# A state-space scan laid out as 8 channels x 16 states per tile instead of 128 channels, and routing counts in two matmuls

## The chip, the cores and the metric

One core of a Trainium2 chip runs the whole program. The metric is the device time of one execution in microseconds (us). The times of the kernel before are three runs: 4642.11, 4643.89 and 4647.07, median 4643.89.

## The reference

A network of four layers on 16 sequences of 256 tokens and 128 channels (4096 tokens). The change is in layer 2, which has two parts. Its first part is a selective state-space block; for a normalised input `xn` of 128 channels:

```python
xz = xn @ W_in; xi, z = jnp.split(xz, 2, axis=-1)          # 256 channels each
xc = silu(causal_conv4(xi) + conv_b)
dt_lo, Bm, Cm = jnp.split(xc @ W_xp, [8, 8 + 16], axis=-1)
delta = softplus(dt_lo @ W_dt + dt_bias)
def step(h, inp):                                          # h: (batch, 256 channels, 16 states)
    dt_t, B_t, C_t, u_t = inp
    h = h * exp(dt_t[..., None] * A) + (dt_t * u_t)[..., None] * B_t[:, None, :]
    return h, einsum('bdn,bn->bd', h, C_t)
y = (scan(step) + xc * D_skip) * silu(z)
out = y @ W_out
```

Its second part is a mixture of 16 experts (128 to 512 to 128, ReLU), two selected per token. The routing gives every token a place in its two experts' rows, for which it counts, per expert, the tokens before it.

## The kernel before

Tokens are worked on in 8 chunks of T = 512 (two sequences of 256). All tensors have channels on the 128 partitions and tokens along the free axis, in float32. The program is written out by hand for five engines (PE, ACT, DVE, POOL and SP for transfers), each with its own in-order list and semaphores between them. It runs layers 0 and 1, then `layer2_route`, `layer2_mix`, and layer 3.

**`layer2_route` (L752)** goes through the chunks in a loop of 9 rounds, one round overlapping the gate and norm of chunk i with the routing of chunk i-1. PE (L834 to L843): `turn(i)`, `logits(i-1)`, the two norm products of chunk i, and last `counts(i-1)` (L821), which counts with 10 products of 16 columns for the tokens before and 4 for the total. DVE (L915 to L932): `select(i-1)`, `gate_finish(i)`, then `place(i-1)` (L893), which waits for the counts, then `ln_vector(i)`. POOL scatters the rows with eight indirect transfers per chunk when the places are there.

**`layer2_mix` (L987)** is the stage of the scan. Each chunk has NS = 16 steps, one per state; the tile of a step is 128 channels x 512 tokens, for two halves of the 256 channels side by side (1024 columns). In every step:

- PE `spread_states(k, n)` (L1072): two products of 32 rows spread row n of B and row n of C over 128 partitions, into banks 0 and 1. They wait for the drive product and C's copy of the step before.
- ACT `decay(k, n)` (L1187): two exponentials exp(delta x A) from SBUF into DA, then C's spread copied from PSUM to CN.
- DVE `drive(k, n)` (L1297): DB = DU x B's spread (out of PSUM, 1024 columns), then the scan (L1308) over 1024 columns.
- POOL (L1355 to L1368): state x C for the near half (L1355), for the far half (L1362), and the far half added up (L1364). DA, DB and ST have two buffers each.
- PE `add_near(k, n-1)` (L1084): a product with the identity adds up the near half in bank 5.

In steps 3 to 12 of a chunk (FIRST = 3, SLOTS = 10) one expert tile of 128 rows runs beside: PE transposes the rows (`tile_rows`, L1099), computes the output of the tile before (`tile_out`, L1113) and this tile's hidden values (`tile_hidden`, L1107), and ACT copies and applies ReLU between them. SP loads the tile j when the output of tile j-2 is done. Each step also carries one part of `head(k+1, n)`: the norm, input projection, convolution, silu, projection to B, C and delta, and the softplus of the next chunk; on ACT, steps 7, 11 and 12 have most of it. The order on every engine is step by step:

```python
for n in range(NS):
    decay(k, n)                                      # ACT; spread_states on PE, drive on DVE
    j = SLOTS * k + n - FIRST
    if FIRST <= n < FIRST + SLOTS: tile_rows(j)
    if FIRST < n <= FIRST + SLOTS: tile_out(j - 1)
    if FIRST <= n < FIRST + SLOTS: tile_hidden(j)
    if k + 1 < CHUNKS: head(k + 1, n)
```

DVE takes the sums of chunk k-1, gates them (`gated`, L1311) after step 0 of chunk k, and adds the input (`add_input`, L1322) after step 1.

`keep_warm` (L125) in other stages issues bf16 products of two constants, `identb` and `windowb`, of 128x128 and 128x512; their result is not read.

Of the kernel before, what the change touches and what calls it, by code (L numbers as in the profile page):

```python
# [13 lines left out]
SEQ = 256  # L14
# [31 lines left out]
def columns(parts):  # L46
    at, out = 0, {}
    for name, width in parts:
# [8 lines left out]
          ("window", 4 * 128), ("expert", E2), ("tile", TILES), ("full", TOKENS // 128), ("eps", 1), ("one", 1), ("aeps", 1), ("pow", 1), ("lnnorm", 1)]  # L57
# [4 lines left out]
W2 = [("g", 1), ("b", 1), ("win", 2 * 2 * 128), ("conv", 2 * TAPS), ("cb", 2), ("xp", 2 * (DTR + 64)), ("dt", DI),  # L62
# [689 lines left out]
def layer2_route(nc, c, w, r, soft, x_mid, s_mid, y_mid, xn_mid, xs_mid, PB):  # L752
    with ExitStack() as ctx:
# [13 lines left out]
        with nc.Block() as block:  # L767
# [31 lines left out]
            def _(pe):  # L799
# [21 lines left out]
                def counts(k):  # L821
                    pe.wait_ge(s.route_ready, k + 1)
                    if k:
                        pe.wait_ge(s.count_taken, k)
                    for t in range(TT):
                        o = PB[:, 6, t * E2:(t + 1) * E2]
                        nc.tensor.matmul(o, c.before, b.OC[:, t, :], start=True, stop=t == 0)
                        for u in range(t):
                            nc.tensor.matmul(o, c.ones, b.OC[:, u, :], start=False, stop=u == t - 1)
                    for t in range(TT):  # L830
                        last = nc.tensor.matmul(PB[:, 6, TT * E2:TT * E2 + E2], c.ones, b.OC[:, t, :], start=t == 0, stop=t == TT - 1)
                    last.then_inc(s.count_ready, 1)

                for i in range(CHUNKS + 1):  # L834
                    if i < CHUNKS:
                        turn(i)
                    if i:
                        logits(i - 1)
                    if i < CHUNKS:
                        pe.wait_ge(s.x_gated, i + 1)  # L840
                        ln_tensor(nc, pe, s, c, of(i).X, PB[:, 1:5], i)
                    if i:
                        counts(i - 1)  # L843
# [22 lines left out]
            def _(dve):  # L866
# [47 lines left out]
                link(nc.vector.tensor_copy(r.base[:], c.expert))  # L914
                for i in range(CHUNKS + 1):  # L915
# [10 lines left out]
                    if i:  # L926
                        place(i - 1)
                    if i < CHUNKS:
# [3 lines left out]
                        ln_vector(nc, dve, s, c, of(i).XN, PB[:, 1:5], link, i).then_inc(s.xn_ready, 1)  # L932

                nc.vector.tensor_scalar(tails[:], r.base[:], 0.0, None, ALU.add).then_inc(s.tails_ready, 1)
# [3 lines left out]
                link(nc.vector.tensor_tensor(b.CT[:], r.base[:], c.expert, ALU.subtract))  # L938
# [41 lines left out]
            "xm_ready xz_ready xi_copied conv_done silu_x silu_z xd_ready dtl_copied bc_copied dt_ready dt_raw dt_exp dt_u dt_log delta_ready "  # L980
            "pads_set b_ready c_ready c_copied drive_ready decay_ready state_ready near_ready far_ready near_added near_summed far_summed "
            "sums_taken y_gated mamba_ready s_added ")
SLOTS = TILES // CHUNKS
FIRST = 3


def layer2_mix(nc, c, w, wf, r, xn_mid, s_mid, xs_mid, ys_mid, PB):  # L987
    with ExitStack() as ctx:
        s = semaphores(nc, ctx, MIX_SEMS)
        b = buffers(nc, ctx, "l2", XN=[3, T], XM=[T], XI=[2, NB, TAPS - 1 + SEQ], XC=[2, 2, T], ZS=[2, 2, T], DL=[2, 2, T], DU=[2, 2, T],  # L990
                    BC=[2, T], EE=[2, T], UU=[2, T], DTL=[T], CN=[2, T], DA=[2, 2, T], DB=[2, 2, T], ST=[2, 2, T],
                    CA=[2, T], CB=[T], YA=[T], YG=[2, T], SO=[T], WB=[2, W2ROW], XR=[2, 128], XT=[128], H=[4, 128], YO=[2, 128])
        xn_loaded, tile_loaded, tile_stored = (s.xn_loaded0, s.xn_loaded1, s.xn_loaded2), (s.tile_loaded0, s.tile_loaded1), (s.tile_stored0, s.tile_stored1)
        B1 = 2 * HID2
        B2 = B1 + 4

        with nc.Block() as block:
            @block.sync
            def _(sp):
# [38 lines left out]
            def _(pe):  # L1038
                def head(k, step):
                    p = k % 2  # L1040
                    if step == 0:
                        pe.wait_ge(xn_loaded[k % 3], 16 * (k // 3 + 1))
                        if k:
                            pe.wait_ge(s.dt_raw, k)
                        nc.tensor.matmul(PB[:, 6, :], c.centre, b.XN[:, k % 3, :], start=True, stop=True).then_inc(s.ln_centred, 1)
                    elif step == 1:
                        pe.wait_ge(s.ln_square, k + 1)
                        nc.tensor.matmul(PB[:, 7, :], c.mean, c.lnsq[:], start=True, stop=True).then_inc(s.ln_var, 1)
                    elif step == 4:
                        pe.wait_ge(s.xm_ready, k + 1)  # L1050
                        for h in range(2):
                            nc.tensor.matmul(PB[:, 6 + h, :], w.win[:, h * 128:(h + 1) * 128], b.XM[:], start=True, stop=True).then_inc(s.xz_ready, 1)
                    elif step == 5:
                        pe.wait_ge(s.xi_copied, k + 1)
                        for h in range(2):
                            nc.tensor.matmul(PB[:, 6 + h, :], w.win[:, (2 + h) * 128:(3 + h) * 128], b.XM[:], start=True, stop=True).then_inc(s.xz_ready, 1)
                    elif step == 9:
                        pe.wait_ge(s.silu_z, 2 * k + 2)
                        pe.wait_ge(s.silu_x, 2 * k + 2)
                        for h in range(2):  # L1060
                            nc.tensor.matmul(PB[0:DTR, 6, :], w.xp[:, h * 72:h * 72 + DTR], b.XC[:, p, h, :], start=h == 0, stop=h == 1)
                        for h in range(2):
# [1013 lines left out]
```

## Time and profile before

| | |
|---|---|
| median of three runs | 4643.89 us |
| profiled execution, its own time | 4658.04 us |
| its span | 4656.4 us |
| mean granted clock of TensorE over the span | 0.793 |
| busy, share of the span | PE 74%, DVE 57%, ACT 39%, POOL 33% |
| layers 0 and 1, up to | about 1120 us |
| `layer2_route` | 1120 to 1347 us |
| `layer2_mix` | 1347 to 2351 us, first scan at 1391.9 |
| layer 3 | from 2351 us |

The profile is of one execution, so its rows are to be held against 4658, not against the median. "Granted clock" is a share of 2.4 GHz; TensorE runs at either 1.2 or 2.4 GHz, and a mean of 0.75 over a stretch is half of it at either. A float32 product appears as two PE instructions, so a count of 8 is four products.

### The profile page before, as it was taken

Reading aid. Unit: us, or ns where it says so; the run is one execution under the profiler, and the core shown is the slowest. Engines: PE = TensorE matmul, PEld = TensorE weight load, DVE = VectorE, ACT = ScalarE, POOL = GpSimd, SP = SyncE. Lnnn points to the kernel's source line nnn. Section 1 sums busy time; section 2 is a strip of 40 time slices with the busy share of each in tenths; the row PEclk is TensorE's granted clock in tenths of the full one; section 3 lists DMA queues with packets and bytes.
Section 4 is the critical chain, followed back from the end, with each engine's and each line's share of the span. In section 5 each row is a group of like instructions: output and inputs, shape, how many; then the busy total and the mean of one; then the engine's idle time right before and its main releaser. Section 6 shows DMA issues by size and latency. Waiting matters only on the chain. (4 is left out here: it accounts for less than half of the span.)

```text
span 4656.4 us, 50785 instructions
## 1 busy us (share of the span) xinstructions
PE 3423.9 (74%) x17802; PEld 1842.6 (40%) x17802; DVE 2642.8 (57%) x3696; ACT 1828.2 (39%) x3692; POOL 1538.3 (33%) x1231
## 2 busy tenths in 40 slices
PE   5888888883538788788757677676776857778587
PEld 3444444441424344344323334333343334343343
DVE  3444444442547777777655566555665656556565
ACT  3333333331214444444424434344343434434344
POOL 0000000003316665656644253332533424334242
PEclk8888888885557777777768879688797988959789
DMA  1000000002212222222100000000000000000000
GB/s 80 7 7 7 7 7 7 7 5 74 72 42 63 67 67 67 67 67 59 59 16 5 8 1 5 8 5 8 1 5 8 5 8 1 8 6 5 8 1 8
DMA packets 70704, 111.46 MB, mean 24 GB/s; under 512 B 8640, under 2 KB 46016, under 8 KB 69952
## 3 DMA queue, kind: packets, MB, share of 16 engines
q1 hardware_dynamic: 65088, 97.47, 6.5%
q0 software_dynamic: 5376, 11.02, 0.9%
q8 instruction: 123, 2.02, 0.2%
q14 instruction: 117, 0.96, 0.1%
HBM read 81.71 MB, written 26.74 MB: 23 GB/s over the span
## 5 line engine op out<-in xcount | busy, mean ns | idle before, releaser
L369 ACT ACTIVATE l_PT<-PB 128x512 f32<-128x512 f32 x512 | 277.9, 594 | 539.1 <-PE PB L280 539.1
L280 PE MATMUL PB<-l_QM,l_KP 32*128 32x256 f32 x2048 | 375.2, 497 | 131.6 <-DVE l_QM L418 75.9
L407 DVE TENSOR_REDUCE keep_MXP<-PB 128x4 f32<-128x1024 f32 x256 | 301.5, 1220 | 106.8 <-PE PB L253 106.8
L280 PEld LDWEIGHTS PB<-l_QM,l_KP 32*128 32x128 f32 x2048 | 241.3, 243 | 256.4 <-ACT l_PT L369 99.9
L1308 DVE TENSOR_TENSOR_SCAN l_ST<-l_DA,l_DB 128x1024 f32<-128x1024 f32 x128 | 313.7, 2451 | 42.0 <-ACT l_DA L1196 32.8
L1355 POOL TENSOR_TENSOR l_CA<-l_ST,l_CN 128x512 f32<-128x512 f32 x128 | 182.6, 1426 | 397.6 <-DVE l_ST L1308 346.0
L703 POOL MEMSET l_KV<- 128x4 f32 x8 | 0.8, 105 | 918.5 <-POOLq L109 918.5
L1515 POOL TENSOR_TENSOR l_PT<-l_PT,l_PEN 128x512 f32<-128x512 f32 x168 | 212.5, 1284 | 184.5 <-ACT l_PT L369 184.5
L1089 PE MATMUL PB<-l_CA,consts 128*128 128x512 f32 x256 | 199.2, 872 | 71.4 <-POOL l_CA L1355 71.4
L1779 POOL TENSOR_TENSOR l3f_SQ<-l3f_RW 128x512 f32<-128x512 f32 x128 | 146.8, 1147 | 302.4 <-ACT l3f_RW L1645 302.4
L1302 DVE TENSOR_TENSOR l_DB<-l_DU,PB 128x1024 f32<-128x1024 f32 x128 | 155.4, 1214 | 154.1 <-PE PB L1079 153.4
L1583 PE MATMUL PB<-l3f_QK 64*64 64x128 f32 x2048 | 159.3, 301 | 80.5 <-DVE l3f_QK L1719 80.5
L1788 POOL TENSOR_TENSOR l3f_PP<-l3f_PP,l3f_RS 128x512 f32<-128x512 f32 x128 | 133.1, 1040 | 251.2 <-DVE l3f_RS L1737 251.2
L1079 PE MATMUL PB<-l_BC,consts 32*128 32x512 f32 x256 | 180.9, 792 | 42.7 <-DVE l_DB L1302 22.0
L253 PE MATMUL PB<-l_KP,l_QP 32*128 32x256 f32 x2048 | 198.0, 514 | 15.6 <-issue 15.6
L1362 POOL TENSOR_TENSOR l_CB<-l_ST,l_CN 128x512 f32<-128x512 f32 x120 | 208.8, 1740 | 0.0
L1670 ACT ACTIVATE l3f_PP<-PB,l3f_MN 128x128 f32<-128x128 f32 x512 | 146.4, 368 | 157.6 <-DVE l3f_MN L1731 157.6
L294 PE MATMUL PB<-l_PT,keep_VT 128*32 128x256 f32 x2048 | 170.6, 490 | 35.2 <-POOL l_PT L1515 19.2
L418 DVE TENSOR_TENSOR l_QM<-l_QP,PB 128x256 f32<-128x256 f32 x128 | 53.9, 421 | 237.0 <-PE PB L262 233.5
L1364 POOL TENSOR_TENSOR l_YA<-l_YA,l_CB 128x512 f32<-128x512 f32 x120 | 184.2, 1535 | 9.4
L1401 POOL TENSOR_SCALAR l_T<-l_AJ,l_GI 128x256 f32<-128x256 f32 x16 | 18.4, 1147 | 504.0 <-DVE l_AJ L1491 504.0
L1081 PE MATMUL PB<-l_BC,consts 32*128 32x512 f32 x256 | 182.1, 797 | 0.0
(416 smaller groups left out, 7934.3 us busy)
## 6 DMA issues: line engine op xcount, KB each, us to landing
l_WB<-in_w2f_dram SPq DMA_DIRECT2D x80, 578.0 KB, 3.4
l_XR<-xs_mid SPq DMA_DIRECT2D x80, 64.0 KB, 3.5
ys_mid<-l_YO SPq DMA_DIRECT2D x80, 64.0 KB, 3.3
w3fs<-in_w3f_dram SPq DMA_DIRECT2D x1, 3125.0 KB, 16.6
keep_XI<-in_x_dram SPq DMA_DIRECT2D x9, 256.0 KB, 3.0
x_mid<-keep_X SPq DMA_DIRECT2D x9, 256.0 KB, 3.0
s_mid<-keep_S SPq DMA_DIRECT2D x9, 256.0 KB, 2.0
keep_SI<-s_mid SPq DMA_DIRECT2D x9, 256.0 KB, 2.6
```

The costliest lines, as they stand in the source:

```text
L253: last = nc.tensor.matmul(PB[:, r, qt * SEQ:(qt + 1) * SEQ], b.QP[rows, a, q0:q0 + 128], b.KP[rows, a, i, sq * SEQ:(sq + 1) * SEQ], start= ...
L280: last = nc.tensor.matmul(PB[:, 4 + u % STBANKS, kt * SEQ:(kt + 1) * SEQ], b.KP[rows, a, i, k0:k0 + 128], b.QM[rows, n % 2, :], start=True ...
L369: nc.scalar.activation(b.PT[:, u % PSLOTS].rearrange("p k q -> p (k q)"), PB[:, 4 + u % STBANKS, :], ACT.Exp).then_inc(s.exp_done, 1)
L407: nc.vector.tensor_reduce(dst[:, 2 * pair:2 * pair + 2, :, 16 + n % 2], PB[:, 2 * pair:2 * pair + 2, :].rearrange("p r (t k) -> p r t k", ...
L1079: nc.tensor.matmul(PB[:, 0, :], c.ident[0:32, n:n + 1].broadcast_to([32, 128]), b.BC[0:32, k % 2, :], start=True, stop=True).then_inc(s.b_ ...
L1081: nc.tensor.matmul(PB[:, 1, :], c.ident[32:64, 32 + n:33 + n].broadcast_to([32, 128]), b.BC[32:64, k % 2, :], start=True, stop=True).then_ ...
L1089: last = nc.tensor.matmul(PB[:, 5, :], c.ident, b.CA[:, g % 2, :], start=n == 0, stop=n == NS - 1)
L1308: nc.vector.tensor_tensor_scan(b.ST[:, g % 2].rearrange("p k t -> p (k t)"), b.DA[:, g % 2].rearrange("p k t -> p (k t)"), b.DB[:, g % 2]. ...
L1355: nc.gpsimd.tensor_tensor(b.CA[:, g % 2, :], b.ST[:, g % 2, 0, :], b.CN[:, g % 2, :], ALU.mult).then_inc(s.near_ready, 1)
L1362: nc.gpsimd.tensor_tensor(b.CB[:], b.ST[:, g % 2, 1, :], b.CN[:, g % 2, :], ALU.mult).then_inc(s.far_ready, 1)
L1364: last = nc.gpsimd.tensor_tensor(b.YA[:], b.YA[:], b.CB[:], ALU.add)
L1515: nc.gpsimd.tensor_tensor(pt, pt, b.PEN[:, 2 * sq:2 * sq + 2, :], ALU.mult).then_inc(s.weighed_pool, 1)
```

## The change

**The scan's layout.** A step now works on a pair of tiles of 8 channels x 16 states (128 partitions) x 512 tokens; 16 pairs (PAIRS) cover the 256 channels. delta and delta x u are spread from 8 channels to 128 partitions by PE (`rowsel`, four products of 32 rows per step: two of delta for the next pair into banks 0 and 1, two of the drive for this pair into banks 2 and 3). B and C are spread once per chunk (`statesel`) and copied to BT and CT by ACT. ACT's exponentials read PSUM. DVE multiplies the drive's spread with BT and scans. POOL makes one product per step, state x CT over 1024 columns in place, in a ring of four buffers, and once per chunk the product delta x xc. PE adds up the 16 states of two pairs with four products of 32 output rows, every second step. Ahead of each step's spreads PE issues FILL = 4 bf16 products of the constants.

```diff
+                def spread(bank, src, k, n, e):
+                    h, i, strip = place(n)
+                    q = 32 * (strip + e)
+                    return nc.tensor.matmul(PB[:, bank + e, :], c.rowsel[q:q + 32, i * 128:(i + 1) * 128],
+                                            src[q:q + 32, k % 2, h, :], start=True, stop=True)
+
+                def spread_pairs(k, n):
+                    g = PAIRS * k + n
+                    ahead = g + 1 < PAIRS * CHUNKS
+                    k1, n1 = divmod(g + 1, PAIRS)
+                    if ahead:
+                        pe.wait_ge(s.decay_ready, g + 1)
+                        if n1 == 0:
+                            pe.wait_ge(s.delta_ready, k1 + 1)
                     if n == 0:
-                        pe.wait_ge(s.bc_copied, k + 1)
+                        pe.wait_ge(s.drive_ready, k + 1)
                     if g:
-                        pe.wait_ge(s.drive_ready, g)
-                        pe.wait_ge(s.c_copied, g)
...
+                        pe.wait_ge(s.drive_done, g)
+                    for _ in range(FILL):
+                        nc.tensor.matmul(PB[:, PAIR0, :], c.identb, c.windowb, start=True, stop=True)
+                    for e in range(2):
+                        if ahead:
+                            spread(0, b.DL, k1, n1, e).then_inc(s.delta_spread, 1)
+                        spread(PAIR0, b.DU, k, n, e).then_inc(s.drive_spread, 1)
+
+                def add_states(k, q):
+                    h, i, _ = place(2 * q)
+                    pe.wait_ge(s.part_ready, PAIRS * k + 2 * q + 2)
+                    if i == 0 and (k or h):
+                        pe.wait_ge(s.y_taken, 2 * k + h)
+                    for n in (2 * q, 2 * q + 1):
+                        for e in range(2):
+                            strip = 2 * (n % 2) + e
+                            last = nc.tensor.matmul(PB[32 * strip:32 * strip + 32, SUMS, :], c.states[:, 24 - 8 * i:56 - 8 * i], b.ST[:, (PAIRS * k + n) % RING, e, :],
+                                                    start=i == 0, stop=i == 3, tile_position=(0, 32 * strip))
+                    last.then_inc(s.y_added, 1)
```

ACT's step, which waits for the spread of delta and no longer copies C, and DVE's:

```diff
+                    for e in range(2):
+                        act.wait_ge(s.delta_spread, 2 * g + e + 1)
+                        group = 16 * h + 4 * (strip + e) + i
+                        last = nc.scalar.activation(b.DA[:, g % 2, e, :].rearrange("p (s t) -> p s t", t=SEQ)[:, :, 1:SEQ],
+                                                    PB[:, e, :].rearrange("p (s t) -> p s t", t=SEQ)[:, :, 1:SEQ],
+                                                    ACT.Exp, scale=c.aneg[:, group:group + 1])
                     last.then_inc(s.decay_ready, 1)
-                    act.wait_ge(s.c_ready, g + 1)
-                    if g >= 2:
-                        act.wait_ge(s.far_ready, g - 1)
-                    nc.scalar.activation(b.CN[:, g % 2, :], PB[:, 1, :], ACT.Copy).then_inc(s.c_copied, 1)
...
+                    dve.wait_ge(s.drive_spread, 2 * g + 2)
+                    nc.vector.tensor_tensor(b.DB[:, g % 2], PB[:, PAIR0:PAIR0 + 2, :], b.BT[:, k % 2, :].unsqueeze(1).broadcast_to([128, 2, T]),
+                                            ALU.mult).then_inc(s.drive_done, 1)
+                    dve.wait_ge(s.drive_done, g + 1)
                     dve.wait_ge(s.decay_ready, g + 1)
-                    if g >= 2:
-                        dve.wait_ge(s.far_ready, g - 1)
...
+                    if g >= RING:
+                        dve.wait_ge(s.y_added, (g - RING) // 2 + 1)
```

POOL's step:

```diff
-                        nc.gpsimd.tensor_tensor(b.CA[:, g % 2, :], b.ST[:, g % 2, 0, :], b.CN[:, g % 2, :], ALU.mult).then_inc(s.near_ready, 1)
...
-                            nc.gpsimd.tensor_tensor(b.CB[:], b.ST[:, g % 2, 1, :], b.CN[:, g % 2, :], ALU.mult).then_inc(s.far_ready, 1)
-                            pool.wait_ge(s.far_ready, g + 1)
-                            last = nc.gpsimd.tensor_tensor(b.YA[:], b.YA[:], b.CB[:], ALU.add)
...
+                        nc.gpsimd.tensor_tensor(b.ST[:, g % RING], b.ST[:, g % RING], b.CT[:, k % 2, :].unsqueeze(1).broadcast_to([128, 2, T]),
+                                                ALU.mult).then_inc(s.part_ready, 1)
+                        if n == 13 and k + 1 < CHUNKS:
+                            drives(k + 1)
```

**What moves with it.** The expert tiles run in steps 5 to 14 (FIRST = 5), and rows, hidden values and projection share bank 5. The head uses one bank (`LANE`) after another instead of two, so each product waits for the copy of the one before: ACT copies the two x halves in steps 3 and 4 (DVE did) and the two z halves in steps 5 and 6 to SBUF, with the silu of z in step 7 over 1024 columns; x projection in one pair of products of 96 columns; delta's bias on ACT in steps 10 and 11 (DVE did), and the add of one in step 11 on ACT; Ln in step 12, where BT is also copied, CT in step 13. The convolutions come one step earlier on DVE (steps 4 and 5), the error term of the softplus in step 11, its end in step 12. DVE takes the first sums of a chunk after step 10 and the second ones, the gate and the input's addition after steps 2 and 3 of the next chunk. `consts` grows by 696 columns.

**Routing.**

```diff
-                    for t in range(TT):
-                        o = PB[:, 6, t * E2:(t + 1) * E2]
-                        nc.tensor.matmul(o, c.before, b.OC[:, t, :], start=True, stop=t == 0)
-                        for u in range(t):
-                            nc.tensor.matmul(o, c.ones, b.OC[:, u, :], start=False, stop=u == t - 1)
...
+                    nc.tensor.matmul(PB[:, 6, 0:TT * E2], c.before, each, start=True, stop=True)
+                    nc.tensor.matmul(PB[:, 6, TT * E2:2 * TT * E2], c.ones, each, start=True, stop=True).then_inc(s.count_ready, 1)
...
                     if i:
                         logits(i - 1)
+                        counts(i - 1)
...
-                    if i:
-                        place(i - 1)
...
                         ln_vector(nc, dve, s, c, of(i).XN, PB[:, 1:5], link, i).then_inc(s.xn_ready, 1)
...
+                    if i:
+                        place(i - 1)
```

`place` now builds the running base of each expert in four additions, one after another, adds it, and copies the last.

## Rows read from the trace of the kernel before

**Rows 1.** Busy time by stretch; after the times: busy us (instructions), clock, DMA.

```profile
core 0: us, PE busy (x) PEld busy (x) DVE busy (x) ACT busy (x) POOL busy (x), PEclk, DMA share, GB/s
1390.00:2331.00 941.00, 748.51 (x2474) 374.41 (x2474) 675.03 (x438) 447.25 (x976) 572.33 (x370) 0.75 0.21 64
1643.00:1714.00 71.00, 63.40 (x240) 34.75 (x238) 50.72 (x37) 37.82 (x91) 42.27 (x30) 0.78 0.28 90
1714.00:1762.00 48.00, 33.59 (x77) 13.54 (x78) 37.51 (x23) 19.33 (x34) 31.15 (x17) 0.65 0.09 30
```

**Rows 2.** Instruction groups, 1330 to 2360 us: busy us, mean ns, idle before, releaser.

```profile
L1308 DVE TENSOR_TENSOR_SCAN l_ST<-l_DA,l_DB 128x1024 f32<-128x1024 f32 x128 | 313.7, 2451 | 42.0 <-ACT l_DA L1196 32.8 <-issue 5.3
...
L1355 POOL TENSOR_TENSOR l_CA<-l_ST,l_CN 128x512 f32<-128x512 f32 x128 | 182.6, 1426 | 397.6 <-DVE l_ST L1308 346.0 <-ACT l_CN L1203 49.5
...
L1302 DVE TENSOR_TENSOR l_DB<-l_DU,PB 128x1024 f32<-128x1024 f32 x128 | 155.4, 1214 | 154.1 <-PE PB L1079 153.4
...
L1270 DVE SCALAR_TENSOR_TENSOR l_XC<-l_XI,w2s,l_XC 128x512 f32<-128x512 f32 x48 | 73.3, 1527 | 1.7
...
L1320 DVE TENSOR_TENSOR l_YG<-l_YG,l_ZS 128x1024 f32<-128x1024 f32 x8 | 17.5, 2194 | 1.2
...
L1250 DVE SCALAR_TENSOR_TENSOR keep_lnt<-PB,consts,keep_lnt 128x512 f32<-128x512 f32 x8 | 6.0, 751 | 0.3
```

**Rows 3.** Timeline, DVE's gate operation L1314, once per chunk: start, duration in us.

```profile
1509.35 0.75 DVE L1314 SCALAR_TENSOR_TENSOR l_YG<-l_XC,w2s,PB 128x512 f32<-128x512 f32 x1
...
2232.20 0.75 DVE L1314 SCALAR_TENSOR_TENSOR l_YG<-l_XC,w2s,PB 128x512 f32<-128x512 f32 x1
...
2341.16 0.75 DVE L1314 SCALAR_TENSOR_TENSOR l_YG<-l_XC,w2s,PB 128x512 f32<-128x512 f32 x1 [5.90 <-PE PB L1089]
```

**Rows 4.** Timeline, one tile step at the full clock.

```profile
1667.70 0.33 PE L1105 MATMUL PB<-consts,l_XR 128*128 128x128 f32 x1 [0.37 <-DMA l_XR<-xs_mid]
...
1669.28 1.16 PE L1110 MATMUL PB<-l_XT,l_WB 128*128 128x128 f32 x8
...
1670.27 1.02 PE L1089 MATMUL PB<-l_CA,consts 128*128 128x512 f32 x2
...
1670.47 1.14 ACT L1214 ACTIVATE l_H<-PB,l_WB 128x128 f32<-128x128 f32 x4 [0.81 <-PE PB L1110]
...
1671.49 1.34 ACT L1196 ACTIVATE l_DA<-l_DL,keep_aneg 128x510 f32<-128x510 f32 x2
...
1674.43 0.33 PE L1105 MATMUL PB<-consts,l_XR 128*128 128x128 f32 x1 [1.90 <-DMA l_XR<-xs_mid]
```

**Rows 5.** Timeline, PE groups: bf16 fills, four strips, expert matmuls at the low clock.

```profile
37.60 1.89 PE L127 MATMUL PB<-windowb,identb 128*128 128x512 bf16 x8
...
46.31 1.15 PE L253 MATMUL PB<-l_KP,l_QP 32*128 32x256 f32 x16
...
1653.78 2.08 PE L1110 MATMUL PB<-l_XT,l_WB 128*128 128x128 f32 x8
```

**Rows 6.** Timeline, ACT's head parts of steps 7 and 12.

```profile
1680.60 1.08 ACT L1164 ACTIVATE l_ZS<-PB 128x512 f32<-128x512 f32 x2
...
1719.76 1.28 ACT L1180 ACT_TABLE_LOAD   x1
1721.05 1.06 ACT L1184 ACTIVATE l_DU<-l_UU 128x1024 f32<-128x1024 f32 x1
```

**Rows 7.** Timeline, a scan and POOL's operations around it.

```profile
1652.36 2.41 DVE L1308 TENSOR_TENSOR_SCAN l_ST<-l_DA,l_DB 128x1024 f32<-128x1024 f32 x1
1652.58 3.25 POOL L1362 TENSOR_TENSOR l_CB<-l_ST,l_CN 128x512 f32<-128x512 f32 x1
...
1657.26 1.26 POOL L1355 TENSOR_TENSOR l_CA<-l_ST,l_CN 128x512 f32<-128x512 f32 x1
```

**Rows 8.** Timeline, counts and placing in one round of the routing.

```profile
1192.04 0.87 PE L827 MATMUL PB<-l2r_OC,consts 128*128 128x16 f32 x4
...
1198.07 0.23 DVE L896 TENSOR_TENSOR l2r_WK<-PB,r_base 128x64 f32<-128x64 f32 x1 [9.71 <-PE PB L831]
...
1200.47 0.42 DVE L153 TENSOR_TENSOR keep_lnt<-keep_lnr 128x256 f32<-128x256 f32 x1
```

More of the change, by code:

```diff
@@ L1043, in head @@
                         if k:
-                            pe.wait_ge(s.dt_raw, k)
-                        nc.tensor.matmul(PB[:, 6, :], c.centre, b.XN[:, k % 3, :], start=True, stop=True).then_inc(s.ln_centred, 1)
+                            pe.wait_ge(s.c_copied, k)
+                        nc.tensor.matmul(PB[:, LANE, :], c.centre, b.XN[:, k % 3, :], start=True, stop=True).then_inc(s.ln_centred, 1)
                     elif step == 1:
                         pe.wait_ge(s.ln_square, k + 1)
[L1048 to L1056, printed above, removed]
@@ new lines, in head @@
+                        if k >= 2:
+                            pe.wait_ge(s.out_taken, SLOTS * (k - 1))
+                        nc.tensor.matmul(PB[:, SMALL, :], c.mean, c.lnsq[:], start=True, stop=True).then_inc(s.ln_var, 1)
+                    elif step == 3 or step == 4:
+                        h = step - 3
+                        if h == 0:
+                            pe.wait_ge(s.xm_ready, k + 1)
+                        else:
+                            pe.wait_ge(s.xi_copied, 2 * k + 1)
+                        nc.tensor.matmul(PB[:, LANE, :], w.win[:, h * 128:(h + 1) * 128], b.XM[:], start=True, stop=True).then_inc(s.xz_ready, 1)
+                    elif step == 5 or step == 6:
+                        h = step - 5
+                        if h == 0:
+                            pe.wait_ge(s.xi_copied, 2 * k + 2)
+                        else:
+                            pe.wait_ge(s.z_copied, 2 * k + 1)
+                        nc.tensor.matmul(PB[:, LANE, :], w.win[:, (2 + h) * 128:(3 + h) * 128], b.XM[:], start=True, stop=True).then_inc(s.xz_ready, 1)
@@ L1057, in head @@
                     elif step == 9:
[L1058 removed]
+                        pe.wait_ge(s.z_copied, 2 * k + 2)
                         pe.wait_ge(s.silu_x, 2 * k + 2)
                         for h in range(2):
[L1061 to L1063 removed]
+                            last = nc.tensor.matmul(PB[0:96, LANE, :], w.xp[:, h * 96:(h + 1) * 96], b.XC[:, p, h, :], start=h == 0, stop=h == 1)
@@ L1092, in project @@
                 def project(k):
                     pe.wait_ge(s.y_gated, k + 1)
-                    pe.wait_ge(s.rows_taken, SLOTS * (k + 1))
+                    pe.wait_ge(s.hid_done, 4 * SLOTS * (k + 1))
                     for h in range(2):
-                        last = nc.tensor.matmul(PB[:, 2, :], w.out[:, h * 128:(h + 1) * 128], b.YG[:, h, :], start=h == 0, stop=h == 1)
+                        last = nc.tensor.matmul(PB[:, WORK, :], w.out[:, h * 128:(h + 1) * 128], b.YG[:, h, :], start=h == 0, stop=h == 1)
@@ L1107, in tile_hidden @@
+                    if j % SLOTS == 0 and k:
+                        pe.wait_ge(s.s_added, k)
+                    nc.tensor.transpose(PB[:, WORK, 0:128], b.XR[:, j % 2, :], c.ident).then_inc(s.rows_ready, 1)
                 def tile_hidden(j):
@@ L2003, in spread_states @@
 def spread_states(a):
[L2005 to L2007 removed]
+    out = np.zeros((a.shape[0], 96), a.dtype)
+    out[:, 0:NS] = a[:, DTR:DTR + NS]
+    out[:, 32:32 + NS] = a[:, DTR + NS:]
+    out[:, 64:64 + DTR] = a[:, 0:DTR]
     return out
```

319 lines of the change are left out of this document (154 added, 165 removed).

## The prediction

> **What bounds the kernel now.** I read the page first (all engines below full: no single one bounds the program), then the busy time by stretch, the groups of the layer 2 stage, and then its timeline, instruction by instruction. The stage in which the edit lies runs from 1390 to 2347 us. There PE is busy 80%, DVE 72%, POOL 61%, ACT 48% [rows 1]: nobody is full, so hand-offs bound it. The reader is to see two things. First, POOL's 1426 ns is a mean over a short and a long case: it takes 1.26 us when DVE lets it, and 3.25 us when a scan of DVE started first [rows 2, 7]. A scan and a POOL operation do not share SBUF; one waits for the other. Second, the chunks with a next head last 120.5 us each ((2232.20 - 1509.35)/6) and the last one, without it, 109 (2341.16 - 2232.20) [rows 3]. Steps that carry an expert tile take 6.7 us where nothing else is in them (1667.70 to 1674.43), there because the tile's rows have not landed [rows 4]; steps with a head part take longer.
>
> **The new step, PE and ACT.** The step's waits now form one closed chain. PE may overwrite the two delta banks only when ACT has made both exponentials of this step; then come the four fills, the four spreads, and behind them in PE's order the tile's transpose, output and hidden matmuls; ACT's relu waits for those, ACT's head part comes behind the relu, and only then ACT's next exponentials. In the kernel before, the exponentials read SBUF and PE did not wait for them. Priced at the full clock: fills 4 x 0.215 = 0.86 (eight bf16 matmuls take 1.89 with 0.17 of drain), spreads 0.86 plus 0.1 to start (16 instructions of 256 columns in four row strips take 1.15 [rows 5]: per strip that is one 512-column product). With 0.03 of hand-over that is 1.85 us from release to the tile's first transpose. From that transpose to the last relu issued it is 3.8 (1667.70 to 1671.49 [rows 4]), then two exponentials 1.1 (now from PSUM; two 512-column ones take 1.08 [rows 6], 1.34 from SBUF). A bare tile step is 1.85 + 3.8 + 1.1 + 0.1 = 6.85, no shorter than the 6.7 that it replaces. C's copy on ACT goes, but into slack.
>
> The page "TensorE: Matmul & The Clock Gate" of the Trainium skill, section "Measured speedup vs the span model", gives four row strips a speedup of 3.07, not 4; by it the spreads would be an estimated 1.12 and the sum some 30 us longer. The trace's row does not agree, and the row is used.
>
> **ACT's heads in that chain.** Each adds its own time to its step: z copies in steps 5 and 6 0.35 and 0.5 (step 5 has no output matmuls before the hidden ones); step 7 two table loads, silus of z and x 4.85; step 9 PE's sums and projection, then a copy 2.0; step 10 0.5; step 11 copy, Abs, Exp and the moved add 4.45 (1.06 per 1024 elements); step 12 tables, Ln and a copy 4.25; step 13 1.2 (tables 1.28, Ln 1.06 [rows 6]; matmul 0.86 + 0.17 [rows 5]). Ten steps are 68.5 + 18.1, and 0.8 more because DVE's two convolutions (six operations at 1.53 [rows 2] when POOL runs beside) hold the drive of steps 6 and 7: 87.4 us.
>
> **The steps without a tile.** Here DVE and POOL bound: the scan is 2.29 and POOL's one operation of 1024 elements twice 1.26 = 2.5, and as they exclude each other a step takes 4.85 with hand-offs, against 1.21 + 2.29 for DVE alone [rows 2, 7]. Steps 15 and 0 are 4.85; step 1 6.15 (mean, Ln, Exp before the exponentials); steps 2 to 4 together 19.55, because DVE does the gate (2.2) and the five layer-norm operations (0.75 each, 3.7) [rows 2] before it is free for the drive of step 3, and ACT's x copy waits for that norm. Sum 35.4. **A chunk at the full clock: 87.4 + 35.4 = 122.8, against 120.5.** POOL's relief (three operations of 512 elements a step to one of 1024) is real and mostly not on the path. The last chunk, without heads, is 10 x 6.85 + 6 x 4.85 = 97.6, against 109 [rows 3].
>
> **The clock.** The granted clock was 0.75 over the stage, 0.78 in tile steps, 0.65 in the others [rows 1]: part of the time at 1.2 GHz, where eight expert matmuls take 2.08 instead of 1.16 [rows 4, 5]. In the new chain all of PE's time of a step counts: 0.86 + 0.86 + 1.58 + 0.99 = 4.3 us (fills, spreads, 1667.70 to 1669.28, 1669.28 to 1670.27) more for a tile step spent at 1.2 GHz, and I take 1 for another step. With a share f of the steps at 1.2 GHz a chunk gains f x 49. The fills make PE denser, but ACT's heads leave PE idle 5 to 7 us after steps 7, 11 and 12, and the part before the next tile, where PE is idle most, had the lower clock before. I take f = 0.3, a granted clock of 0.85: between the 0.78 of before and full, as nothing in the trace has both fills and such gaps. Bounds: 0 and 0.6.
>
> **Routing.** PE's counts sit between the last rstd and DVE's placing: from 1192.04 to 1198.07, then 2.4 of placing to 1200.47 [rows 8]. Both leave that path; the placing comes back behind the norm with four more linked operations (2.4 + 1.0). Net 5.0 x 7, 4 on the last count: -40 (bounds -25 to -45: at least the count goes; at most the placing is hidden too). POOL's scatters start when the placing is done, and wait longer than they work, so they stay hidden. Constants: 356 KB more in the first loads, +2, if they are on the path at all. First head of the stage, alone: one bank instead of two serialises copies and the drive product goes to POOL, +4. SP's order does not change; its loads of a tile land 5.1 us behind the output matmuls (1669.3 to 1674.43 [rows 4]), inside 6.85 and little more.
>
> **Sum.** At f = 0.3: chunk 122.8 + 14.7 = 137.5, 7 x 17 = +119; last chunk 97.6 + 14.7 against 109, +3; routing -40; +6. Together +88, on the profiled execution's 4658.0 us (its span is 4656.4): 4746; the median of the runs is 4643.9, 14 below, so **4732 us**. At f = 0.16 it is 4677, at 0.44 4787. A measurement of this kernel tells about 0.2% (9 us) from no change.
>
> **Rivals.**
> (1) The fills hold the clock at full. Then f = 0: 7 x 2.3 - 11 - 34 = -29: 4615, faster. It decides where PE's gaps stop lowering the clock, below f = 0.07. For it: bf16 fills of the full array sit in front of all 128 steps. Against it: the gaps behind ACT's heads are longer than the steps. The Trainium skill ("TensorE: Matmul & The Clock Gate", "What's actually happening") says that the default is the low rate and activity releases it; by that rule this is where it would end if the fills suffice. Chance 0.17.
> (2) The chain of ACT and PE is looser than I have it and only the shared SBUF path of DVE and POOL bounds: 16 x 4.8 + 16.3 of DVE's head work + 2.5 of POOL's = 95.6 a chunk; 7 x -25 - 32 (16 x 4.8 against 109) - 34 = -241: 4403. For it: the old excess over 3.5 us of DVE per step went with POOL's load. Against: the order in the code. Chance 0.12.
> (3) The clock sinks: f = 0.6, chunk 152, 4850. For it: in the part with few tiles the clock averaged 0.65 with PE busy 70% of the time [rows 1]. Against it: this is where the fills help most. Chance 0.13.
> (4) The four spreads do not run side by side, since a product is two instructions each and PE issues in order: 2.6 us more in 128 steps, +330, over 5000. Against it the 1.15 for 16 [rows 5]. Chance 0.03.
> (5) Small gains and losses cancel, within 0.2%: 0.05.
>
> **How the numbers follow.** My own case (4677 to 4787) has 0.50. Faster: (1), (2) and none of mine, 0.29, with a little more for routing, 0.30. Same 0.05. Slower 0.65. The range 4590 to 4860 takes in (1) and (3), and leaves out (2), (4) and tails of (1) and (3), 0.2.
>
> **What would show it.** Right: POOL's share in the stage falls by a third and yet DVE idles, released by PE's drive spread; PE waits for ACT's exponentials in tile steps; ACT waits for hidden matmuls; tile steps 7 us bare, 11 to 12 where silu, Abs or Ln is in them; the four spreads in about 1.1 us at full clock; granted clock 0.8 to 0.9; chunks 130 to 144; routing rounds 24 -> 19. Wrong: chunks under 118, or a scan that starts every 4.8 us in tile steps (rival 2), or a clock above 0.95 (rival 1), or spreads lasting over 2 us at the full clock (rival 4).

## The result and the profile after

The changed kernel takes 4780.8 us (median of 4 runs, 4775.7 to 4794.3) beside 4645.5 us for the kernel before (4 runs, 4642.1 to 4658.9): ratio 1.029, 95% interval 1.026 to 1.032, slower. Forecast: 4732, range 4590 to 4860, slower with 0.65. Only fast runs are compared, none over 1.5% above the fastest of its kernel: this leaves out one of 8615 us in e5 and two of 6337 and 4800 us in e7.

In the profiled execution the span is 4776.1 us against 4656.4, +119.7. By the starts of the first scan and of the last addition of the input, the part ahead of the first scan is 34.1 shorter (1357.8 against 1391.9), the scan stage 153.2 longer (to 2467.0, 1109.1, against 955.9), the rest equal (2309.1 and 2308.4 by stretch).

Busy time by stretch of the changed kernel: the stage, one chunk with a next head, and the last gate to gate. They answer to [rows 1].

```profile
core 0: us, PE busy (x) PEld busy (x) DVE busy (x) ACT busy (x) POOL busy (x), PEclk, DMA share, GB/s
1357.00:2455.00 1098.00, 756.62 (x3739) 340.26 (x3738) 598.29 (x397) 416.30 (x895) 317.47 (x134) 0.86 0.18 55
1660.76:1804.10 143.34, 98.55 (x474) 43.93 (x474) 76.94 (x52) 54.50 (x115) 40.28 (x18) 0.86 0.18 55
2368.20:2461.90 93.70, 68.78 (x398) 35.09 (x398) 51.56 (x31) 30.35 (x84) 32.28 (x14) 0.91 0.23 67
```

POOL's 572 us of before are 317 and DVE's 675 are 598, as the layout promises; POOL's share of the stage falls from 61% to 29%, more than the third that was forecast. The stage gains nothing by it: all four engines now idle more. The groups of the stage say for what they wait; they answer to [rows 2].

```profile
L1401 POOL TENSOR_TENSOR l_ST<-l_ST,l_CT 128x1024 f32<-128x1024 f32 x128 | 303.7, 2373 | 788.3 <-DVE l_ST L1346 788.3
L1346 DVE TENSOR_TENSOR_SCAN l_ST<-l_DA,l_DB 128x1024 f32<-128x1024 f32 x128 | 296.9, 2320 | 4.4
L1111 PE MATMUL PB<-windowb,identb 128*128 128x512 bf16 x508 | 160.7, 448 | 315.5 <-ACT l_DA L1256 300.6 <-DVE l_DB L1340 14.9
L1340 DVE TENSOR_TENSOR l_DB<-PB,l_BT 128x1024 f32<-128x1024 f32 x128 | 156.5, 1223 | 438.5 <-PE PB L1095 438.2
L1270 ACT ACTIVATE l_H<-PB,l_WB 128x128 f32<-128x128 f32 x320 | 91.2, 367 | 69.3 <-PE PB L1148 69.3
```

Read in a ring: POOL waits 788 us for the scan; the scan waits for its drive product just ahead of it; the drive waits 438 us (154 before) for the spreads L1095; PE waits 301 us ahead of the fills L1111 for ACT's exponentials L1256; and ACT waits for the tile's matmuls (transpose to copy 266, hidden to relu 69). That is the closed chain. The chunk's mark is now DVE's gate product L1356 (it stands two steps later in a chunk than before):

```profile
1517.50 2.84 DVE L1356 TENSOR_TENSOR l_YG<-l_YG,l_ZS 128x1024 f32<-128x1024 f32 x1
...
2368.20 2.85 DVE L1356 TENSOR_TENSOR l_YG<-l_YG,l_ZS 128x1024 f32<-128x1024 f32 x1
...
2461.86 1.22 DVE L1356 TENSOR_TENSOR l_YG<-l_YG,l_ZS 128x1024 f32<-128x1024 f32 x1
```

A chunk lasts (2368.20 - 1517.50)/6 = **141.8 us** against the 120.5 of [rows 3]. One bare tile step of the last chunk at the full clock, in the timeline:

```profile
2403.62 0.33 PE L1143 MATMUL PB<-consts,l_XR 128*128 128x128 f32 x1
...
2406.38 1.14 ACT L1270 ACTIVATE l_H<-PB,l_WB 128x128 f32<-128x128 f32 x4 [0.81 <-PE PB L1148]
...
2407.39 1.27 ACT L1256 ACTIVATE l_DA<-PB,keep_aneg 128x510 f32<-128x510 f32 x2
...
2408.72 1.04 PE L1111 MATMUL PB<-windowb,identb 128*128 128x512 bf16 x4 [2.38 <-ACT l_DA L1256]
2409.69 0.69 PE L1095 MATMUL PB<-l_DL,consts 32*128 32x512 f32 x1
...
2410.78 0.33 PE L1143 MATMUL PB<-consts,l_XR 128*128 128x128 f32 x1
```

7.16 us from transpose to transpose: 3.77 to the exponentials, 1.33 until the fills, 0.97 of fills, 1.09 of spreads. The four spreads (eight instructions) run side by side; the line shown is the first of them. And step 11, with a long part of the next head, where the clock has fallen:

```profile
1883.34 1.14 ACT L1270 ACTIVATE l_H<-PB,l_WB 128x128 f32<-128x128 f32 x4 [0.81 <-PE PB L1148]
1885.38 0.69 ACT L1229 ACTIVATE l_DL<-PB,w2s 128x512 f32<-128x512 f32 x1 [0.91 <-PE PB L1082]
1886.10 1.06 ACT L1232 ACTIVATE l_EE<-l_DL 128x1024 f32<-128x1024 f32 x1
1887.19 1.06 ACT L1233 ACTIVATE l_EE<-l_EE 128x1024 f32<-128x1024 f32 x1
1888.28 1.15 ACT L1234 ACTIVATE l_UU<-l_EE,consts 128x1024 f32<-128x1024 f32 x1
1889.33 1.24 ACT L1256 ACTIVATE l_DA<-PB,keep_aneg 128x510 f32<-128x510 f32 x2
...
1890.63 1.89 PE L1111 MATMUL PB<-windowb,identb 128*128 128x512 bf16 x4 [5.29 <-ACT l_DA L1256]
```

PE stands idle 5.3 us while ACT works on the *next* chunk (Abs, Exp and the add of one, L1232 to L1234). The four fills then take 1.89 us, as long as eight did at the full clock [rows 5]. This step lasts 15.05 us from scan to scan.

### The profile page after: what moved, and what is told of

It reads as the page before. It is cut to its first block and busy times, and to the rows that moved or that the text cites. A ratio compares the mean times of both kernels' runs of the same rounds, so it can differ in the third digit from the quotient of the medians.

```text
span 4776.1 us, 52386 instructions
## 1 busy us (share of the span) xinstructions
PE 3400.5 (71%) x18890; PEld 1773.0 (37%) x18890; DVE 2563.4 (54%) x3680; ACT 1802.2 (38%) x3620; POOL 1274.5 (27%) x991
## 5 line engine op out<-in xcount | busy, mean ns | idle before, releaser
L1401 POOL TENSOR_TENSOR l_ST<-l_ST,l_CT 128x1024 f32<-128x1024 f32 x128 | 303.7, 2373 | 788.3 <-DVE l_ST L1346 788.3
L280 PE MATMUL PB<-l_QM,l_KP 32*128 32x256 f32 x2048 | 359.6, 480 | 131.8 <-DVE l_QM L418 76.0
L1340 DVE TENSOR_TENSOR l_DB<-PB,l_BT 128x1024 f32<-128x1024 f32 x128 | 156.5, 1223 | 438.5 <-PE PB L1095 438.2
L1111 PE MATMUL PB<-windowb,identb 128*128 128x512 bf16 x512 | 162.6, 449 | 316.3 <-ACT l_DA L1256 301.3
L280 PEld LDWEIGHTS PB<-l_QM,l_KP 32*128 32x128 f32 x2048 | 233.1, 234 | 248.2 <-ACT l_PT L369 97.7
L1346 DVE TENSOR_TENSOR_SCAN l_ST<-l_DA,l_DB 128x1024 f32<-128x1024 f32 x128 | 296.9, 2320 | 4.4
L1111 PEld LDWEIGHTS PB<-windowb,identb 128*128 128x128 bf16 x512 | 44.0, 106 | 453.7 <-ACT l_DA L1256 412.8
L1095 PE MATMUL PB<-l_DL,consts 32*128 32x512 f32 x512 | 196.0, 843 | 0.0
L294 PE MATMUL PB<-l_PT,keep_VT 128*32 128x256 f32 x2048 | 169.7, 488 | 35.7 <-POOL l_PT L1551 25.6
L1095 PE MATMUL PB<-l_DU,consts 32*128 32x512 f32 x512 | 194.0, 839 | 0.0
L1256 ACT ACTIVATE l_DA<-PB,keep_aneg 128x510 f32<-128x510 f32 x256 | 161.4, 687 | 38.3 <-PE PB L1095 29.0
L1619 PEld LDWEIGHTS PB<-l3f_QK 64*64 64x64 f32 x2048 | 132.5, 155 | 114.6 <-issue 111.4
```

What stands on the lines that cost most here:

```text
L280: last = nc.tensor.matmul(PB[:, 4 + u % STBANKS, kt * SEQ:(kt + 1) * SEQ], b.KP[rows, a, i, k0:k0 + 128], b.QM[rows, n % 2, :], start=True ...
L294: last = nc.tensor.matmul(PB[32 * r:32 * r + 32, 7, 0:SEQ], VT[:, 2 * sq + kt, 8 * a + 2 * r + i, :], b.PT[:, (NR * (2 * j + i) + r) % PSL ...
L1095: return nc.tensor.matmul(PB[:, bank + e, :], c.rowsel[q:q + 32, i * 128:(i + 1) * 128], src[q:q + 32, k % 2, h, :], start=True, stop=True)
L1111: nc.tensor.matmul(PB[:, PAIR0, :], c.identb, c.windowb, start=True, stop=True)
L1256: last = nc.scalar.activation(b.DA[:, g % 2, e, :].rearrange("p (s t) -> p s t", t=SEQ)[:, :, 1:SEQ], PB[:, e, :].rearrange("p (s t) -> p ...
L1346: nc.vector.tensor_tensor_scan(b.ST[:, g % RING].rearrange("p k t -> p (k t)"), b.DA[:, g % 2].rearrange("p k t -> p (k t)"), b.DB[:, g % ...
```

## The experiments

The theory is the closed chain of the prediction: the exponentials come behind relu and head on ACT, PE's spreads behind the exponentials, the tile's matmuls behind the spreads. Its rivals: fills and clock set the time; the SBUF path shared by DVE and POOL sets it; the routing hides or adds something. A chunk is measured from gate to gate, as above, over six chunks, or between two neighbouring gates where a stretch is named. The diffs are shortened.

**Routing alone (e1), and the change without it (e8).**

```diff
-  (before) 14 count products a round, counts and placing ahead of the norm
+  (e1)     two products over OC as [128, TT*E2]; counts and placing behind the norm
```

> The routing's counts and placing alone, on the scan of before. My theory: about 42 us less than before (seven rounds of 24.0 become 18.7, the last saves 4 to 5), 4603. Rival, that the routing's gain is given back behind it (POOL's scatters, the zero rows): less than 20 us gained.

Measured: 4624.3 us, ratio 0.998 (0.991 to 1.005); the median is 13 below before and the interval too wide to tell that from nothing. Yet the first scan starts at 1341.8, 50.1 earlier. The profiled executions say where it went. In the scan stage, whose code is that of before, a chunk takes 116.3 us where it took 120.5, and the stage ends 75.5 earlier. Behind it the time is lost: the stretches behind the last addition of the input, first before, then e1, with the same 10096 matmuls.

```profile
2348.00:4656.40 2308.40, 1678.90 (x10096) 894.71 (x10096) 1381.00 (x2089) 945.34 (x1904) 843.74 (x729) 0.83 0.02 6
```
```profile
2272.30:4639.90 2367.60, 1738.91 (x10096) 928.41 (x10096) 1379.41 (x2089) 945.19 (x1904) 844.93 (x729) 0.80 0.02 6
```

In e1 the granted clock of layer 3 was 0.80, not 0.83, and that code, which no edit touches, took 59 us longer. So neither expectation can be told by the whole time, and runs of whole kernels that differ by under some 40 us are read by stage here.

> The change without its routing part: the scan as changed, the counts of the routing as they were before. If the routing rounds are on the path for their full length and nothing else moves (5 rounds of 23.95 instead of 18.68 us and what goes with them, 44 to 50 us between the changed and the old start of the mix stage): 4820 to 4832 us. Rival, that the clock's swings of later stages eat it, as e1's median of -13 us might be read: 4780 to 4800 us.

Measured: 4831.1 us, ratio 1.044 (1.038 to 1.049), 50 over the changed kernel; its first scan starts at 1387.9, 30 later than with the new routing. That is the first expectation. The routing stage itself tells it best: from the first placing to the last it takes 161.5 us before and in e8, 120.1 and 120.0 in the changed kernel and in e1. So the new routing is worth 41 us. The rest of the 30 to 50 is in code that is the same: among the changed kernel and its variants with the same routing the first scan starts anywhere from 1352.5 (e3) to 1376.6 (e4).

**No fills (e2).**

```diff
-FILL = 4
+FILL = 0
```

> The changed kernel without the four fills. Chain theory: 0.95 us off each tile step at the full clock and less in the others, some 90 us, but the granted clock of the stage falls; if it falls by 0.1 or more the gain is eaten and the time is 4780 or above. Rival, the fills do nothing for the clock: 4690, clock of the stage unchanged.

Measured: 4747.2 us, ratio 1.026 (1.020 to 1.032), 139.7 us per chunk. This is neither expectation: the clock of a chunk sinks from 0.86 to 0.72, which was to give 4780 or more, and the time is 34 us below the changed kernel's. The chunk is 2 us *shorter*: the fills hold the clock, and behind the wait for the exponentials their own 1 to 1.9 us a step cost a little more than the clock gives.

**Fills ahead of the wait (e3).**

```diff
 def spread_pairs(k, n):
+    if g: pe.wait_ge(s.drive_done, g)
+    for _ in range(FILL): ...
     if ahead: pe.wait_ge(s.decay_ready, g + 1)
-    if g: pe.wait_ge(s.drive_done, g)
-    for _ in range(FILL): ...
```

> The same fills, but ahead of the wait for ACT's exponentials instead of behind it, so that they run while PE would wait. Chain theory: they leave the closed chain and still keep the clock: 1 to 1.9 us less per step, 100 to 150 us less, 4630 to 4680. Rival, DVE and POOL bound the stage: no change.

Measured: 4668.2 us, ratio 1.008 (1.003 to 1.014), 129.8 us per chunk. The same work takes 113 us less than in the changed kernel, as the chain theory has it, because it is done while PE would wait. The group of the spreads now carries the wait, and it is half of what it was:

```profile
L1095 PE MATMUL PB<-l_DL,consts 32*128 32x512 f32 x512 | 185.1, 798 | 152.9 <-ACT l_DA L1256 152.8
L1105 PE MATMUL PB<-windowb,identb 128*128 128x512 bf16 x512 | 153.9, 430 | 47.7 <-DVE l_DB L1340 47.7
```

**The exponentials ahead of the relu (e4).** On ACT alone:

```diff
+                decay(0, 0)
 for n in range(PAIRS):
-    decay(k, n)
     tile_rows(j); tile_out(j - 1)
+    decay(*divmod(PAIRS * k + n + 1, PAIRS))
     tile_hidden(j); head(k + 1, n)
```

> ACT makes the exponentials of the next step between the expert tile's copies and its relu, not behind relu and head part. The spread that they read is there since the step's start. Chain theory: ACT's 1.25 us and the fills, spreads of the next step no longer wait for relu and head: tile steps 6.9 to 9, 100 to 200 us less, 4580 to 4680, and PE's wait for the exponentials is gone. Rival, shared SBUF path of DVE and POOL: no change. Second rival, the tile's loads (5.1 us behind its output) bound at once: under 60 us gained.

Measured: **4521.5 us, ratio 0.976 (0.971 to 0.981)**, 107.2 us per chunk: 259 us less than the changed kernel and, by 1.9 to 2.9%, faster than the kernel before. That is more than I expected (100 to 200). The groups of its stage:

```profile
L1348 DVE TENSOR_TENSOR_SCAN l_ST<-l_DA,l_DB 128x1024 f32<-128x1024 f32 x128 | 340.6, 2661 | 4.4
L1403 POOL TENSOR_TENSOR l_ST<-l_ST,l_CT 128x1024 f32<-128x1024 f32 x128 | 314.4, 2458 | 512.6 <-DVE l_ST L1348 512.6
L1342 DVE TENSOR_TENSOR l_DB<-PB,l_BT 128x1024 f32<-128x1024 f32 x128 | 155.8, 1218 | 146.0 <-PE PB L1095 144.3
L1111 PE MATMUL PB<-windowb,identb 128*128 128x512 bf16 x508 | 140.6, 401 | 80.8 <-DVE l_DB L1342 41.9 <-ACT l_DA L1256 38.1
```

DVE's wait for the spreads falls from 438 to 144 us, PE's for the exponentials from 301 to 38. The clock of six chunks rises from 0.86 to 0.94 on the same four fills (they take 401 ns, not 448): with shorter gaps on PE more of its time is at the higher clock. Most of the gain is not the clock's: e6 (below), the same order without fills and at a clock of 0.77, takes 198 us less than e2.

The edit takes two things off the chain, relu and the next chunk's head. By the starts of the scans a chunk loses 34.9 us, and 23.3 of them are in the four steps with ACT's longest head parts, 7, 11, 12 and 13 (52.5 us together in the changed kernel, 29.2 in e4). The bare step 8 loses nothing (7.14 and 7.43 us): behind relu the next bound is close. There PE waits for the tile's rows, which it did not in the changed kernel:

```profile
L1143 PE MATMUL PB<-consts,l_XR 128*128 128x128 f32 x80 | 27.1, 339 | 37.4 <-DMA l_XR<-xs_mid 37.1
```

So the second rival of the expectation, the tile's loads, holds for bare steps, but not for the stage.

**Both (e5), and e4 without fills (e6) or e5 with eight (e11).**

> The changed kernel with ScalarE's exponentials of the next step ahead of the relu (as in e4) and the four fills issued before PE waits for them (as in e3). Closed-chain theory: e4 already took the exponentials off the path, so the fills wait for them only 39 us in all in e4's profile; moving the fills too gives 0 to 40 us more, 4480 to 4520 us, 102 to 107 us per chunk. Rival, that each of the two edits removes its own part (113 and 259 us): near 4410 us, under 95 us per chunk.

Measured: 4513.2 us, ratio 0.973 (0.967 to 0.980), 106.4 us per chunk. This is within 9 us of e4 and far from 4410: the two edits break the same chain, and do not add.

> As e4 (exponentials ahead of the relu), and without any fill products. Theory that the fills pay for themselves by holding TensorE's clock: granted clock of the mix stage falls from e4's 0.91 to 0.75 to 0.85, and as the tile steps are now bound by PE's work at full clock, the time is 4530 to 4600 us, slower than e4. Rival, that the fills are only a cost of 1.04 us per step on PE: up to 128 x 1.04 = 133 us less than e4, near 4400 us; e2 against the changed kernel (-33 us, clock 0.86 to 0.72) lies between the two.

Measured: 4548.8 us, ratio 0.980 (0.975 to 0.985), 111.0 us per chunk with clock 0.77. It is slower than e4 by 27 us, 3.8 a chunk, as the clock theory has it: with the chain open the fills lie mostly in idle time, and now they earn.

> e5 (exponentials ahead of the relu, fills ahead of the wait for them) with eight fill products a step in place of four. Four more cost 4 x 0.215 = 0.86 us of PE a step at full clock. Theory that PE's order bounds most steps and the clock is at 0.93 already: +50 to +110 us, 4565 to 4625 us. Rival, that the rest of the clock is worth more than that, or that the fills fit into PE's idle time: 4480 to 4515 us.

Measured: 4541.3 us, ratio 0.980 (0.972 to 0.987), 108.6 us per chunk. That is 28 us over e5, a quarter of the PE time added (128 x 0.86 = 110), and so below my range, and not the rival's gain either, although the granted clock of the chunks is now 1.00 (0.95 in e5): the last twentieth of the clock is worth less than the fills that hold it. Of none, four and eight, four is best.

**Half of POOL's product (e7, e10).** Both leave out the product with C for the second tile of each pair.

```diff
-tensor_tensor(ST[:, g % RING], ST[:, g % RING], CT ... [128, 2, T])
+tensor_tensor(ST[:, g % RING, 0:1], ST[:, g % RING, 0:1], CT ... [128, 1, T])
```

> The changed kernel, GpSimd multiplies only the first tile of each pair with C, so the second tile's sum takes the bare states (half of its product is left out, 128 x 1.19 us = 152 us of GpSimd's work). Closed-chain theory: GpSimd's product is behind the scan and nobody on the chain waits for it: 4755 to 4790 us, 140 to 142 us per chunk. Rival, that the path shared by VectorE and GpSimd sets the pace: 4630 us, near 123 us per chunk.

Measured: 4730.4 us (two runs), ratio 1.021 (1.014 to 1.027), 50 us under the changed kernel. That is below my range, and my 140 to 142 a chunk is a miss too: it is 135.8 where the changed kernel takes 141.8. So the shared path does not set the pace (that would have been 123 a chunk and 4630 us), but it costs some 6 us a chunk, a part of them by the clock, which is 0.90 in e7's chunks and 0.86 in the changed kernel's. (The profiled execution took 4800.2 us; behind the stage it took 2370.6 us at a clock of 0.79, in code that no edit touches.) DVE's lines, first of the changed kernel, then of e7 (duration in ns min/median/max, first to last start):

```profile
L1346 DVE TENSOR_TENSOR_SCAN l_ST<-l_DA,l_DB x128: 2290/2291/3423, 1357.8 to 2454.2; 128x1024 f32<-128x1024 f32 x128
...
L1356 DVE TENSOR_TENSOR l_YG<-l_YG,l_ZS x8: 1224/2843/2851, 1517.5 to 2461.9; 128x1024 f32<-128x1024 f32 x8
...
L1340 DVE TENSOR_TENSOR l_DB<-PB,l_BT x128: 1192/1224/1226, 1356.6 to 2453.0; 128x1024 f32<-128x1024 f32 x128
```
```profile
L1356 DVE TENSOR_TENSOR l_YG<-l_YG,l_ZS x8: 1225/1757/1766, 1519.0 to 2422.8; 128x1024 f32<-128x1024 f32 x8
```

> e4 (exponentials ahead of the relu) with GpSimd multiplying only the first tile of each pair (the second tile's product with C is left out). Theory that with the chain of ScalarE gone the path shared by VectorE and GpSimd is next: the scans fall from 2.66 to about 2.3 us (128 x 0.37 = 47 us) and head parts by 3 to 5 us a chunk: 4430 to 4485 us. Rival, that PE's own order (tile step 7 us) bounds: 4500 to 4525 us, with the scans shorter all the same.

Measured: 4483.8 us, ratio 0.968 (0.961 to 0.975), 38 under e4, the scans at 2368 ns instead of 2661, the stage's clock 0.98. This is the first expectation, at the edge of its range. With ACT's chain open, the path of DVE and POOL is a bound, but mostly in the steps without a tile, which give 5.7 of the 8.0 us a chunk; tile steps go from 68.2 to 65.9. How much of the 38 is the clock's (0.93 in e4) was not separated.

**The old scan with the fills (e9).**

```diff
 def spread_states(k, n):
     ...
+    for _ in range(4): matmul(PB[:, 0, :], identb, windowb)
     matmul(PB[:, 0, :], ...)   # B
```

> The old layout of the scan (128 channels, 16 states), with the changed routing as in e1 and four bf16 fill products ahead of each step's two spreads. Asks how much of e4's gain needs the new layout. Theory that the fills alone bring little, since what they give the clock they take from PE (e2, e6): within 40 us of e1, 4585 to 4660 us. Rival, that the higher granted clock is what makes e4 fast and the layout adds nothing: granted clock of the mix stage near 0.9 and 4500 to 4550 us.

Measured: 4643.9 us (10 runs), ratio 1.003 (0.999 to 1.007), 20 over e1, and 120.1 us per chunk for 116.3. That is the first expectation. Over the stage, first e9, then e5:

```profile
1342.00:2290.00 948.00, 785.99 (x2940) 378.26 (x2987) 690.80 (x445) 452.80 (x979) 594.76 (x376) 0.86 0.21 64
```
```profile
1355.00:2213.40 858.40, 694.12 (x3750) 320.91 (x3750) 650.16 (x398) 405.43 (x893) 365.58 (x135) 0.93 0.23 70
```

The clock rises to 0.86 here too (0.76 in e1) and buys nothing. So what makes e4 and e5 fast is neither the clock nor the routing but the new layout with what moves with it, once its chain is open. POOL's 595 us are 366 in it; what each part of that change is worth by itself, the head's single bank and the operations moved to ACT above all, no run separates.

## Why the prediction was right, and where it was off

**The closed chain** held as written in the tile steps. Each of its hand-overs is in the trace of after, and moving one link (e4) took 259 us away, with all of the change's work left in.

**A chunk** was put at 137.5 and measures 141.8. The table adds up the steps by the starts of the scans, mean of chunks 1 to 6, in us. The forecast is at the full clock; its clock term adds 12.9 to the tile steps and 1.8 to the others.

| steps | forecast, full clock | with its clock term | changed kernel | e7 | e4 |
|---|---|---|---|---|---|
| 15, 0 and 1 | 15.85 | 16.75 | 16.9 | 16.9 | 14.7 |
| 2 to 4 | 19.55 | 20.45 | 25.6 | 22.0 | 24.4 |
| 5 to 14 (a tile) | 87.4 | 100.3 | 99.7 | 97.7 | 68.2 |
| sum | 122.8 | 137.5 | 142.2 | 136.5 | 107.3 |

**The term that was mis-sized** is that of steps 2 to 4: 25.6 for 20.45, which is the whole miss. In steps 2 and 4 DVE works without a gap. The prediction let the two convolutions hold the drives of steps 6 and 7, for 0.8 us. In the code they stand in steps 4 and 5, and each holds the next drive. Step 4 alone takes 8.2 us where 4.85 was its base:

```profile
1961.99 2.29 DVE L1346 TENSOR_TENSOR_SCAN l_ST<-l_DA,l_DB 128x1024 f32<-128x1024 f32 x1
1964.19 0.52 DVE L1317 TENSOR_SCALAR l_XC<-l_XI,w2s 128x512 f32<-128x512 f32 x1
1964.75 4.29 DVE L1319 SCALAR_TENSOR_TENSOR l_XC<-l_XI,w2s,l_XC 128x512 f32<-128x512 f32 x3
1968.95 1.22 DVE L1340 TENSOR_TENSOR l_DB<-PB,l_BT 128x1024 f32<-128x1024 f32 x1
```

Step 3 takes 7.0 us for 4.85: ACT's x copy stands ahead of its exponentials, and the fills and spreads behind them run at the lower clock (3.6 us together).

**Right by luck, in two places.** Steps 15 and 0 were put at 4.85 because DVE's scan and POOL's product would exclude each other. They take 5.16 and 4.98, but not for that reason: with POOL's product halved (e7) they stay at 5.16 and 4.98, and DVE's drive waits for the spreads there too, so the closed chain bounds them:

```profile
1931.50 1.22 DVE L1340 TENSOR_TENSOR l_DB<-PB,l_BT 128x1024 f32<-128x1024 f32 x1 [1.61 <-PE PB L1095]
```

And the tile steps come out right in sum, 99.7 for 100.3, though the **bare tile step** was put at 6.85 and measures 7.16: the rows to the exponentials were right (3.8, measured 3.77); exponentials with hand-over 1.33 for 1.2, fills 0.97 for 0.86, spreads 1.09 for 0.99. Over ten steps that is 3.1 us too few, which the other terms hide in the sum.

The Trainium skill's "TensorE: Matmul & The Clock Gate", section "Measured speedup vs the span model", gives four row strips a speedup of 3.07. The prediction used the row, and the traces bear the row out, not the page: from 1882.84 to 1883.98 in e4, four 32-row products of 512 columns take 1.14 us, and one alone (L1085, both of its instructions) 1.12.

```profile
1882.84 0.69 PE L1095 MATMUL PB<-l_DL,consts 32*128 32x512 f32 x1
...
1883.39 0.59 PE L1095 MATMUL PB<-l_DU,consts 32*128 32x512 f32 x1
...
1887.33 1.12 PE L1085 MATMUL PB<-l_BC,consts 32*128 32x512 f32 x2
```

**The clock** was taken as 0.85 and was 0.86 over the stage and over a chunk. It falls behind the long heads, as the prediction had it (0.74 in step 11, 0.80 in steps 2 to 4). **The heads** came close: step 11 takes 15.05 us for 11.3 at full clock plus up to 4.3.

**First and last chunk.** From the first scan to the first gate product (L1320 before, L1356 after) it is 159.7 us for 121.7, and from the last but one to the last 93.7 for 106.2: +37.9 and -12.6, where the forecast had +17 and +3. Most of both is one slip of bookkeeping: the gate moved two steps later, so some 16 to 21 us go from the last stretch to the first. Of the sum, 25 for 20, the rest is open.

**Routing** was put at -40. A round takes 18.7 for 24.0 us, and from the first placing to the last it is 120.1 for 161.5, -41.4. With the other terms ahead of the first scan (+6) the forecast was -34, and -34.1 was measured. That it fits to a tenth is luck: in kernels with the same code up to there the first scan starts anywhere within 24 us.

**Sum.** Measured +119.7 in the profiled executions and +135 in the medians, forecast +88. Of the 32 between +88 and +120 the chunks are 6 x 4.3 = 26, and 5 are in the first and last.

**The rivals.** (1), full clock, fell: it was 0.86, and e2 shows that the fills paid nothing where they stood. Nearly full clock came in e10 (0.98), on the same four fills and with shorter gaps, and in e11 (0.99), on eight. (2), the shared path alone, fell as the bound of this kernel: the scans start mostly 7 to 15 us apart in tile steps. It is a bound once the chain is open (e10), and e4's 107 us a chunk lies between it and mine. I had not counted that it takes up to 6 us of each chunk even here: in e7 each of steps 2, 4 and 5, with the gate's product and the convolutions, is 1.1 us shorter. (3), a sinking clock, fell: it was 0.86. (4), strips one after the other, fell: the four take 1.09 us.

## What to carry to other kernels

When an operation's input moves from a buffer in SBUF to a PSUM bank that TensorE refills each step, that operation joins TensorE's chain: put it ahead of everything on its engine that TensorE needs only later, here ahead of relu and of the next chunk's work. Where TensorE has a long wait, issue work that only keeps the clock ahead of it, not behind it: that was worth 113 us here, and nothing that can be measured once the wait was gone. And measure a small gain by its stage: here unchanged code behind it moved by up to 70 us with the granted clock.

## What the runs showed of the hardware that I had not expected

- The granted clock of an unchanged stage varies between executions of nearly the same program: layer 3 took 2298 us at 0.83 in e5 and 2368 at 0.80 in e1.
- DVE and POOL collide only in some operations. DVE's scan, with both inputs in SBUF, stretches from 2.29 to 3.42 us beside POOL (never in e7, with POOL's product halved), and the gate's product from 1.22 to 2.85 (1.77 in e7); the drive product L1340, with one input in PSUM, never takes over 1.226 us in 128 times. The Trainium skill's "GPSIMD Engine Reference", section "1. Specifications", says that the two engines contend when VectorE's instruction has two SBUF inputs; the trace agrees.
- From 1871 to 1879 us PE was busy 6.07 of 8 us at a granted 0.97, and over the next 15 us, step 11 with its 5.3 us of waiting, the granted clock was 0.73: at 1.2 GHz from 1880 to 1882, ahead of that wait, at 2.4 GHz from 1882, and at 1.2 GHz again from 1890 to 1894. So the clock fell twice, and the first time PE's idle times just before had been under 2 us each. I had expected the four fills of each step to count for more.
